# x of the expert tiles transposed in 32x32 blocks by VectorE instead of by TensorE, from tiles loaded by quarters of the columns

## What is computed

```python
    x = x + _L0_attn_ref(_layernorm(x), ...)
    x = x + _L0_ffn_ref(_layernorm(x), ...)

    def _L0_ffn_ref(hidden_states, router_w, e_bias, gate_up_proj, down_proj, ...):
        scores = jax.nn.sigmoid(x @ router_w.T)
        _, topk_idx = jax.lax.top_k(scores + e_bias[None, :], TOP_K)
        ...
        def step(acc, xs):
            gu_w, d_w, c = xs
            g, u = jnp.split(x @ gu_w.T, 2, axis=1)
            y = jax.nn.silu(g) * u @ d_w.T
            return (acc + c[:, None] * y, None)
        routed, _ = jax.lax.scan(step, jnp.zeros_like(x), (gate_up_proj, down_proj, combine.T))
        shared = jax.nn.silu(x @ shared_gate_w.T) * (x @ shared_up_w.T) @ shared_down_w.T
        return routed + shared
```

## Time and profile before

| | |
|---|---|
| runs, median (lowest to highest) | 1956.91 us (1956.83 to 1957.64), 3 runs |
| the profiled execution, its time | 1947.51 us |
| its span | 1945.6 us |
| granted PE clock over the span | 0.985 |
| copy of the transposed x, ACT L1700, 128x512 | 595 ns, x176 |
| Silu, ACT L1706, 128x192 | 330 ns, x176 |
| hidden, DVE L1850, mean of its forms | 348 ns, x216 |
| copy of y, ACT L1716, 128x512 | 595 ns, x166 |
| indirect add, POOL L1647, its issue | 1551 ns, x72 and x72 |

### The profile page before, as it was taken

How to read it: one execution, slowest core, us unless ns; L and a number is a source line. 1 busy time by engine, 2 the same in 40 slices (tenths; PEclk the granted TensorE clock), 3 DMA queues, 4 the chain that set the end, 5 groups by cost and what they waited for, 6 DMA issues and landing times. The chain is left out here.

```text
span 1945.6 us, 34872 instructions
## 1 busy us (share of the span) xinstructions
PE 1872.0 (96%) x9240; PEld 965.8 (50%) x9241; DVE 1031.1 (53%) x1995; ACT 978.7 (50%) x1901; POOL 921.2 (47%) x1127
## 2 busy tenths in 40 slices
PE   6899999999999999999999899999999999999996
PEld 5444445444544454445333455555555555555553
DVE  5667777878787878787888252222221222222213
ACT  3366776677667766776766532223332233322330
POOL 3533566666666766675633650333333333333342
PEclk9799999999999999999999999999999999999998
DMA  6422334434443444333532897877777777777779
GB/s 193 108 70 64 83 94 132 128 107 116 132 134 103 116 131 135 104 103 120 150 120 82 290 342 237 183 142 141 141 144 142 142 141 141 143 143 141 142 164 262
DMA packets 159128, 277.71 MB, mean 143 GB/s; under 512 B 28704, under 2 KB 64800, under 8 KB 156256
## 3 DMA queue, kind: packets, MB, share of 16 engines
q1 hardware_dynamic: 108688, 147.61, 26.7%
q0 software_dynamic: 40880, 106.96, 26.6%
q10 hardware_dynamic: 9440, 21.68, 3.2%
HBM read 145.65 MB, written 135.74 MB: 145 GB/s over the span
## 5 line engine op out<-in xcount | busy, mean ns | idle before, releaser
L993 DVE TENSOR_REDUCE mx<-ps_max 128x2 f32<-128x1024 f32 x512 | 618.1, 1219 | 174.7 <-PE ps_max L1203 160.6
L732 ACT ACTIVATE prob<-ps_exp 128x512 f32<-128x512 f32 x992 | 566.9, 598 | 149.2 <-PE ps_exp L1217 131.6
L1948 PE MATMUL ps_gu<-wts_sb,xT 128*128 x1152 | 402.7, 493 | 1.2 <-issue 1.0
L1217 PE MATMUL ps_exp<-qs,ks 98*128 98x512 bf16 x992 | 380.0, 383 | 18.9 <-ACT prob L732 16.7
L1647 POOL DMA_INDIRECT out<-yt,idx x72 | 111.7, 1551 | 467.6 <-ACT yt L1716 453.2
L1203 PE MATMUL ps_max<-ks,qs 96*128 96x512 bf16 x1024 | 310.2, 385 | 7.5 <-DVE mx L993 4.0
L1828 DVE COPY hT<-ps_h 128x384 f32<-128x384 f32 x88 | 49.1, 557 | 463.2 <-PE ps_h L1957 463.2
L1948 PEld LDWEIGHTS ps_gu<-wts_sb,xT 128*128 128x128 f32 x1152 | 207.3, 190 | 170.9 <-issue 56.4
L1245 PE MATMUL ps_pv<-prob,vs 128*32 128x512 f32 x2048 | 251.8, 605 | 0.2 <-ACT prob L740 0.2
L1706 ACT ACTIVATE gs<-ps_gu 128x192 f32<-128x192 f32 x176 | 58.2, 330 | 376.4 <-PE ps_gu L1948 376.4
L1217 PEld LDWEIGHTS ps_exp<-qs,ks 98*128 98x128 bf16 x992 | 96.8, 98 | 195.7 <-ACT prob L732 88.5
(11 more groups left out here) (197 smaller groups left out, 2177.2 us busy)
## 6 DMA issues: line engine op xcount, KB each, us to landing
xt<-rows_by_expert SPq DMA_DIRECT2D x144, 264.5 KB, 2.7
dnr_sb<-in_dnr SPq DMA_DIRECT2D x144, 128.0 KB, 2.6
qk_parts<-parts POOLq DMA_DIRECT2D x112, 120.0 KB, 3.6
qs<-qk_parts SPq DMA_DIRECT2D x64, 192.0 KB, 3.1
wts_sb<-in_wts ACTq DMA_DIRECT2D x12, 1024.0 KB, 8.3
x_sb<-in_x SPq DMA_DIRECT2D x16, 512.0 KB, 4.5
qs<-qk_parts SPq DMA_DIRECT2D x64, 128.0 KB, 3.1
x_plus_memory<-am SPq DMA_DIRECT2D x16, 512.0 KB, 5.2
```

The source lines that it names most:

```text
L732: act.activation(prob[:, s, q], ps_exp[:, q % 2], ACT.Exp, scale=SCALE).then_inc(s_exp, 1)
L993: dve.tensor_reduce(mx[:, k % 2, 4 * s + 2 * p:4 * s + 2 * p + 2], ps_max[:, p], AX_X, ALU.max).then_inc(s_maxd, 1)
L1217: pe.matmul(ps_exp[:, q % 2], ks[0:ROWS + MROWS, kk, s * P:(s + 1) * P], qs[0:ROWS + MROWS, kk, q], start=True, stop=True).then_inc(s_sc, 1)
L1948: mm = pe.matmul(ps_gu[:, i, 0:2 * I], xT[:, i, d], w, start=(d == 0), stop=(d == DC - 1))
```

## The change

x of a tile no longer comes whole. Four DMAs bring quarter a of the columns (128 of 512) into partitions 32a to 32a+31, with the 128 rows as four blocks of 32 side by side; each run is 512 bytes. VectorE then transposes the tile in 32x32 blocks with one instruction, straight into xT in SBUF. The contraction index that a partition of xT holds is another one than before, and the gate-up weights are laid out for it on the host. The weights and token of each row come in a fifth DMA into a tile of their own, xw (17 f32 a row). PE's transposes, ACT's copies, their PSUM banks and s_xp are gone. From pair 12 on, tile 1 of the later pair is loaded by ACT's queue between the two Silus. VectorE transposes tile i of the following pair behind hidden of tile i, and reads weights and tokens at the start of its body. PE reads the numbers of the experts of the pair before just ahead of down.

```diff
-    xt = lent("xt", [P, 4, RW])
+    xt = lent("xt", [P, 4, D])
...
+    def load_quadrants(eng, pair, i, rows):
+        for a in range(QD):
+            part = slice(a * QD_ROWS, (a + 1) * QD_ROWS)
+            eng.dma_start(xt[part, pair.slot(i)].rearrange("t (b d) -> t b d", b=QD),
+                          rows[:, a * P:(a + 1) * P].rearrange("(b t) d -> t b d", t=QD_ROWS)).then_inc(s_x[pair.slot(i)], 16)
+    def load_tile(eng, pair, i):
+        if pair.kind == SHARED:
+            load_quadrants(eng, pair, i, XN2[bass.ds(pair.t[i], 1)].rearrange("o p d -> (o p) d"))
+        else:
+            row = eng.value_load(tab[0:1, 0, bass.ds(pair.j[i], 1)], min_val=0, max_val=ZERO_ROW)
+            eng.dma_start(xw[:, pair.slot(i)], XS[bass.ds(row, P), D:RW]).then_inc(s_xw[pair.slot(i)], 16)
+            load_quadrants(eng, pair, i, XS[bass.ds(row, P), 0:D])
+    def on_act(later):
+        return not isinstance(later.h, int) or later.h >= H0 + 2
...
         def load_x(pair):
-            for i in range(2):
...
+            for i in range(1 if on_act(pair) else 2):
+                load_tile(sp, pair, i)
...
-                wait(s_xp, 2 * pair.h + 2)
+                wait(s_xT, 2 * pair.h + 2)
...
     def scalar(act):
-        def x_out(pair):
-            for i in range(2):
-                act.wait_ge(s_xp, 2 * pair.h + i + 1)
-                after(act.wait_ge, s_gu, 2 * pair.h + i - 1)
-                act.activation(xT[:, i], ps_x[:, i], ACT.Copy).then_inc(s_xT, 1)
...
             silu(pair, 0)
             last_units(chain, pair, "a")
+            if later.exists and on_act(later):
+                act.wait_ge(s_xT, 2 * pair.h + 2)
+                act.sem_inc(s_acg, 1)
+                if pair.kind == ROUTED:
+                    act.wait_ge(s_tok, pair.routed + 1)
+                    act.sem_inc(s_acg, 1)
+                load_tile(act, later, 1)
             silu(pair, 1)
-            if following.exists:
-                x_out(following)
...
+        def x_out(pair, i):
+            dve.wait_ge(s_x[pair.slot(i)], 16 * QD * (pair.q + 1))
+            after(dve.wait_ge, s_gu, 2 * pair.h + i - 1)
+            dve.transpose(xT[:, i].rearrange("p c (b t) -> p c b t", b=QD),
+                          xt[:, pair.slot(i)].rearrange("p (b c d) -> p c b d", b=QD, c=DC)).then_inc(s_xT, 1)
...
                 last.then_inc(s_h, 1)
+                if following.exists:
+                    x_out(following, i)
...
         def body(before, pair, following, later):
+            if pair.kind == ROUTED:
+                weights(pair)
+                tokens(pair)
             if before.exists:
                 hT_out(before)
...
     def tensor(pe):
-        def transpose_x(pair):
...
-                for d in range(DC):
-                    mm = pe.transpose(ps_x[:, i, d], xt[:, slot, d * P:(d + 1) * P], identf[:])
-                mm.then_inc(s_xp, 1)
...
-            e_before, e = experts(before), experts(pair)
+            e = experts(pair)
...
-            if following.exists:
-                transpose_x(following)
             if before.exists:
-                down(before, e_before)
+                down(before, experts(before))
...
-            gu.transpose(2, 0, 1).reshape(DC, P, E, 2 * I).transpose(1, 2, 0, 3).reshape(P, E, -1),
+            gu.transpose(2, 0, 1).reshape(QD, DC, QD_ROWS, E, 2 * I).transpose(0, 2, 3, 1, 4).reshape(P, E, -1),
```

More of the change, by code:

```diff
@@ L32 @@
 DC = D // P
+QD_ROWS = 32
+QD = P // QD_ROWS
 SEQ = 512
@@ L1382, in feed_forward @@
     sgu_sb, sdn_sb, sdnr_sb = (keep[k] for k in ("sgu", "sdn", "sdnr"))
+    xw = keep["xw"]
     token, idx, wpick, wsel, tab, small, smi, padf, padi = (keep[k] for k in (
@@ L1387, in feed_forward @@
     wts_sb = lent("wts_sb", [P, E, W])
-    xt = lent("xt", [P, 4, RW])
-    lent("room_in_x_sb", [P, 6 * D - 4 * RW])
+    xt = lent("xt", [P, 4, D])
+    lent("room_in_x_sb", [P, 2 * D])
     xT = lent("xT", [P, 2, DC, P])
@@ L1407, in feed_forward @@
     jt = room[:, NR * (E + 3):NR * (E + 9)].rearrange("p (k j) -> p k j", k=6)
-    ps_x = own.enter_context(nc.psum_tensor("ps_x", [P, 2, DC, P], F32))
     ps_y = own.enter_context(nc.psum_tensor("ps_y", [P, 2, D], F32))
@@ L1421, in feed_forward @@
     s_x = [sem(f"f_x_loaded{r}") for r in range(4)]
+    s_xw = [sem(f"f_x_weights_loaded{r}") for r in range(4)]
     s_dn = [sem(f"f_down_rest_loaded{p}") for p in range(2)]
-    s_xp = sem("f_xT_in_psum")
     s_xT = sem("f_xT")
@@ L1764, in scalar @@
                 act.sem_inc(s_acg, 1)
-        x_out(Pair(0, 0, 0))
         pairs(act, body)
@@ L1828, in hT_out @@
             dve.tensor_copy(hT[:], ps_h[:, 0:3]).then_inc(s_hT, 1)
+        def x_out(pair, i):
[3 more added lines that the diff above has]
+                          xt[:, pair.slot(i)].rearrange("p (b c d) -> p c b d", b=QD, c=DC)).then_inc(s_xT, 1)
         def weights(pair):
             for i in range(2):
-                dve.wait_ge(s_x[pair.slot(i)], 16 * pair.q + 16)
-            dve.tensor_tensor(wpick[:], xt[:, 2 * pair.par:2 * pair.par + 2, CW:CW + E],
+                dve.wait_ge(s_xw[pair.slot(i)], 16 * (pair.q - H0 // 2) + 16)
+            dve.tensor_tensor(wpick[:], xw[:, 2 * pair.par:2 * pair.par + 2, 0:E],
                               onehot[:, bass.ds(pair.j[0], 2)], ALU.mult).then_inc(s_wp, 1)
@@ L1838, in weights, with hidden @@
             dve.wait_ge(s_wp, 2 * pair.routed + 2)
-        def hidden(pair):
+        def hidden(pair, following):
             for i in range(2):
@@ L1853, in hidden @@
                 last.then_inc(s_h, 1)
+                if following.exists:
+                    x_out(following, i)
         def tokens(pair):
             dve.tensor_copy(token[:, 2 * pair.par:2 * pair.par + 2],
-                            xt[:, 2 * pair.par:2 * pair.par + 2, TOK].bitcast(U32)).then_inc(s_tok, 1)
+                            xw[:, 2 * pair.par:2 * pair.par + 2, E].bitcast(U32)).then_inc(s_tok, 1)
         def add_at(pair):
@@ L1883, in body @@
             last_units(chain, pair, "a")
-            if pair.kind == ROUTED:
-                weights(pair)
-            hidden(pair)
+            hidden(pair, following)
             last_units(chain, pair, "b")
-            if pair.kind == ROUTED:
-                tokens(pair)
             if before.exists and before.kind == ROUTED:
@@ L1912, in vector @@
                 dve.sem_inc(s_dvg, 1)
+        for i in range(2):
+            x_out(Pair(0, 0, 0), i)
         pairs(dve, body)
@@ L1993, in tensor @@
                 pe.wait_ge(s, n)
-        transpose_x(Pair(0, 0, 0))
         pairs(pe, body)
@@ L2076, in kept @@
             "smi": sb("smi", [P, E], I32), "padf": sb("padf", [P, E]), "padi": sb("padi", [P, E], U32),
-            "sgu": sb("sgu_sb", [P, DC, 2 * I]), "sdn": sb("sdn_sb", [P, D]), "sdnr": sb("sdnr_sb", [P, D])}
+            "xw": sb("xw", [P, 4, RW - D]), "sgu": sb("sgu_sb", [P, DC, 2 * I]), "sdn": sb("sdn_sb", [P, D]), "sdnr": sb("sdnr_sb", [P, D])}
 def kernel(L0_attn_x, L0_attn_Wq, L0_attn_Wk, L0_attn_Wv, L0_attn_memory, L0_attn_memory_norm, L0_attn_memory_weight,
@@ L2107 @@
         "wts": np.ascontiguousarray(np.concatenate([
-            gu.transpose(2, 0, 1).reshape(DC, P, E, 2 * I).transpose(1, 2, 0, 3).reshape(P, E, -1),
+            gu.transpose(2, 0, 1).reshape(QD, DC, QD_ROWS, E, 2 * I).transpose(0, 2, 3, 1, 4).reshape(P, E, -1),
             dn[:, 0:P].transpose(1, 0, 2)], axis=2)),
         "dnr": np.ascontiguousarray(dn[:, P:I]),
-        "sgu": chunks(np.concatenate([np.asarray(L0_ffn_shared_gate_w), np.asarray(L0_ffn_shared_up_w)]).T),
+        "sgu": np.ascontiguousarray(np.concatenate([np.asarray(L0_ffn_shared_gate_w), np.asarray(L0_ffn_shared_up_w)]).T.reshape(
+            QD, DC, QD_ROWS, 2 * I).transpose(0, 2, 1, 3).reshape(P, DC, 2 * I)),
         "sdn": np.ascontiguousarray(sdn[0:P]),
```

## The result

The changed kernel took 1891.97 us (median of 4 runs, 1890.37 to 1893.8) against 1957.28 us for the kernel before on the same chip (1956.83 to 1960.67): ratio 0.9663, 95% interval 0.9646 to 0.968, 65.3 us less. The prediction was 1892.2 us. Its profiled execution took 1893.8 us, of which 1892.0 are the span.

A forecast was written before the change was run, and what follows sets the result against it. PE was taken to bound the routed stage, DMA the stretches before and after it; -63.5 (transposes), -2.5 (early stage) and +1.3 (tail) gave -64.7 us, hence 1892.2 us, range 1881 to 1918.

The forecast's parts named there:

- PE loses the transposes: Routed stage: 73 pair bodies each lose eight PE transposes of x, 0.87 us, so 63.5 us off.
- VectorE's transposes cost nothing: Each pair: two block transposes of 0.69 us on VectorE stay hidden, with 3 us of cover even at the upper end.
- ScalarE's load of tile 1 costs nothing: Between ScalarE's two Silus: one register read and five issues, 2.6 us, delay nothing.
- SyncE's 4.6 us of 8.47: SyncE's (SP's) queue: issues for tile 0 and the remaining down weights take 4.6 us of the 8.47 us pair, costing nothing.
- PE's moved reads cost nothing: Just before down: two expert-number reads, 1.1 us, hide behind gate-up 1's 2.58 us of queued matmuls.
- rival (d): Before down in routed pairs: the moved reads stall PE, 79 us on against 64.7 off, 1971 us; chance 0.02.
- DMA work: Routed pair: 512-byte packets at 36 ns make 124.2 engine-us, 7.8 us of 16 engines, under 8.47.
- rival (c): Load queues: every 512-byte packet waits behind an adds packet, 64 ns, pair 9.55 us, slower at 1989 us; chance 0.04.
- (b): Load queues: transfers bind part of the gain, packets of 54 ns, pair 8.9 us, 1936 us in all; chance 0.12.
- The early stage, 2.5 us kept: Stage before 1195 us: x lands net 1.2 us later, so 2.5 us kept of the 8.7 ten pairs would give.
- The tail, +1.3: After 1888.2 us: four tiles loaded there add 1.3 us; 5 at 64 ns.
- The sum: Whole kernel: -63.5 - 2.5 + 1.3 = -64.7 us, profiled execution 1882.8, plus 9.4 to the runs' median, 1892.2 us.

The follow-up runs named there:

- the doubled x: Changed kernel with each routed pair loading both x tiles again into a tile nothing reads, compared with the kernel before: 1987.27 us, ratio 1.0194.
- the control: The changed kernel without any edit, run again beside three edited kernels and compared with the kernel before on that chip: 1885.56 us, ratio 0.9701.

## Why the prediction was right, step by step

*PE loses the transposes*: -63.5 foreseen, -64.8 measured from pair 10 to 82, and shown by their return (9.34 us a pair, 63.0 us more in that stage, 67.8 between the medians). Of the 64.8, 72 pairs of 0.87 are 62.6; most of the rest is 1.7 us that the kernel before lost in this stage beside its pairs (674.2 us against 72 x 9.34 = 672.5), 1.0 of it waits of PE. The pair of 8.47 us was read from the kernel before's last pairs.

*VectorE's transposes cost nothing*: right. 0.69 us was taken, 702 ns measured, and x of tile 0 is done 4.6 us after gate-up 0's start (4.9 foreseen), of tile 1 at 8.0 (7.3). The estimate of 1.24 us from the Trainium skill (VectorE: DVE Perf Modes, The three transpose paths), four times its 311 ns for bf16, would be too high by three quarters: the row decides.

*ScalarE's load of tile 1 costs nothing*: right; its issues are a median 372 ns, not 420.

*SyncE's 4.6 us of 8.47*: nothing lost, but the term was too small. A tile takes 3.25 us of the queue and the down weights' rest 3.8, so about 7 us of 8.47; in the changed kernel's own trace the queue waits 18.8 of 100 us, 1.6 a pair, which leaves 6.9. The estimate counted the issues and one read, and not what the queue spends between them. Its consequence was missed: with a second tile on that queue the kernel would have been slower than before, and no rival said so.

*PE's moved reads cost nothing; rival (d)*: right, and the other side of it was missed. Left where they were they cost 9.6 us in the routed stage (619.0 against 609.4).

*DMA work*: the price of 36 ns was right (34 by the doubled x); rival (c)'s 64 ns is refuted, (b)'s 54 too. The sum of 124.2 engine-us a pair came out as 111.1. Of the 13 us, 7 are the adds' queue, whose packets are busy 55.8 engine-us a pair (41.2% x 16 x 8.46) in place of 63.1 (42.2% x 16 x 9.34) for the same work. That fits the prediction's suspicion that the shares count waiting; what the packets wait for is not shown. The other 6 are in the load queues, 55.4 in place of the sum's 61.1. The Trainium skill's rule to join transfers under 64 KB (DMA: Bandwidth & Descriptors, Rules for kernel authors) did not decide here: ten small loads a pair fit in 8.47 us as long as two queues issue them. It is the queue's issuing that is short, as SyncE's alone showed. The 2.0 us a transfer that the prediction took from the Trainium skill (DMA: Bandwidth & Descriptors, Anatomy of one DMA) are a fit for transfers that GpSimd issues; these come from SyncE and ScalarE.

*The early stage, 2.5 us kept*: this step is not borne out. The two first profiles give 5.2 us lost and 2.9 more before pair 0. Of what comes before pair 0 the prediction had 0.5; the pairs of profiles give 2.9 and, on the second chip, 4.3 to 5.0. In the first two profiles PE's wait for pair 0's x explains 1.4 of the 2.9 (1.66 us in place of 0.25, VectorE's attention work standing ahead of the transposes); the rest is open. Over the four profiles whose schedule up to pair 10 is that of the changed one (104.5, 97.0, 100.0 with the reads back, 99.4 with one queue) the mean is 100.2, and the kernel before has 99.3 and 102.6: against that scatter neither a gain nor a loss can be told. What the sum got wrong is to treat the landing in one execution as fixed; it moves by more than the term. That DMA work is what holds it is borne out: the share is 0.98, and with less of it in that stretch PE is busy longer.

*The tail, +1.3*: +3.2 in the first profiles, within its end of 5; the tail is 62.0 to 63.6 us in all profiles with the change and 60.3 and 59.7 without. The transfers themselves are 0.9 longer, near the term. What the prediction had wrong is where the tail begins. It read 1888.2 us as the end of the last routed pair's down projection; that is pair 82's, of the shared expert, and pair 81's ended at 1878.9. What GpSimd waits for is the landing of pair 81's adds, 9.4 us later, and this was counted neither as a part of the path nor as something that the change could make later (10.8 us after it). The 73 bodies are right all the same, since they end with pair 81's down projection.

*The sum*: -64.7 foreseen for a profile-to-profile difference that was -53.6, and for medians that differ by 65.3. That the median came out to 0.3 us is in part luck: against the first two profiles the early term was 10.6 us too good, the tail 1.9, the routed stage 1.3 too cautious, 11.2 together; and the profiled execution of before lay 9.4 us under the median that the forecast starts from, that of after 1.8 above its own, which makes 11.2 on the other side. On the later chip the control gained 57.9 us (ratio 0.9701), at which the forecast would have been 7 us too low. The range, 1881 to 1918 or a gain of 39 to 76 us, covered this.

## What to carry to other kernels

Where PE is full and the pair is a closed chain, read the shorter pair off the trace itself, then ask of each queue that takes new work how long its whole round is, the time between the issues included: SyncE's was at 7 of 8.47 us and one tile more would have turned the gain into a loss. A register read or an issue that is free in the old pair is to be priced anew in the shorter one. And take no term from the stretch that differs most between runs of the same kernel without a second profile of it.

## What was not expected of the hardware

VectorE transposes 128x512 f32 in 32x32 blocks in 702 ns on average (672 to 712, 176 of them), 2% above an elementwise operation of that size (687 ns). After PE had waited 2.6 to 4.9 us, the next gate-up took 4.5 to 5.5 us in place of 2.8. The granted clock was 0.55 and 0.50 over the two shown above, so most or all of each ran at the lower of its two levels (1.2 GHz), and the wait cost PE up to 2.7 us more than its length. And SyncE's queue takes 3.25 us for a tile's five transfers, whose issue instructions are 2.2 us together (0.35 + 1.83).
